# Expert tiles from the thirteenth on as float16 pairs, with the weights split on the chip

## The reference

```python
def attention(xn, Wq, Wk, Wv, Wb, Wg, Wo, norm_w):      # 4 heads, DK 128, DV 64
    q, k, v = xn @ Wq, xn @ Wk, xn @ Wv
    beta = sigmoid(xn @ Wb)
    k = k * rsqrt(sum(k * k) + 1e-12); q = q * SCALE
    # per token: pred = k_t S; S += k_t (beta_t (v_t - pred)); o_t = q_t S
    o = delta_rule(q, k, v, beta)
    o = o * rsqrt(mean(o * o) + 1e-5) * norm_w * silu(xn @ Wg)
    return o @ Wo

def ffn(xn, router_w, expert_fc, expert_proj):          # 8 experts, hidden 1024
    e = argmax(softmax(xn @ router_w.T))                # one expert for a token
    h = square(relu(xn @ expert_fc[e]))
    return h @ expert_proj[e].T

out = x + attention(xn) * silu(ffn(xn))
```

## Time and profile before

| | |
|---|---|
| median of 3 runs | 779.52 us (777.28 to 780.23) |
| profiled execution, its own time | 778.46 us |
| its span, first to last instruction | 776.7 us |
| TensorE busy | 729.9 us, 94% |
| VectorE busy | 537.6 us, 69% |
| GpSimd busy | 359.7 us, 46% |
| ScalarE busy | 356.5 us, 46% |

### The profile page before, as it was taken

How to read it: one execution, slowest core, us unless ns; L and a number is a source line. 1 busy time by engine, 2 the same in 40 slices (tenths; PEclk the granted TensorE clock), 3 DMA queues, 4 the chain that set the end, 5 groups by cost and what they waited for, 6 DMA issues and landing times.

```text
span 776.7 us, 22979 instructions
## 1 busy us (share of the span) xinstructions
PE 729.9 (94%) x9442; PEld 625.4 (81%) x9442; DVE 537.6 (69%) x1137; ACT 356.5 (46%) x768; POOL 359.7 (46%) x380
## 2 busy tenths in 40 slices
PE   5986999999999999999999999999999999999996
PEld 4764888878888788887978878888888888979873
DVE  6998156565665666646666586867777767777788
ACT  5922435444454444544445444444444353535532
POOL 5745126355353553535535272636354544426431
PEclk9988999999999999999999999999999999999999
DMA  8517853334433344333543333333333333323157
GB/s 295 182 55 271 301 191 150 149 130 151 190 132 135 131 176 173 142 118 130 193 154 144 116 138 110 130 117 124 124 124 123 123 124 123 118 110 118 36 179 263
DMA packets 37753, 116.33 MB, mean 150 GB/s; under 512 B 3664, under 2 KB 24400, under 8 KB 27664
## 3 DMA queue, kind: packets, MB, share of 16 engines
q1 hardware_dynamic: 33904, 104.62, 36.3%
q0 software_dynamic: 3744, 10.23, 4.2%
HBM read 101.33 MB, written 13.50 MB: 148 GB/s over the span
## 4 chain that ended last, share of the span: by engine, by line
PE 78%; DVE 11%; issue 4%; ACT 3%; DMA 2%; POOL 1%; DVEq 0%; SPq 0%; POOLq 0%
PE bank L521 18%; PE bank L510 16%; PE bank L556 5%; PE bank L590 5%; PE bank L484 4%; PE bank L486 4%; PE bank L485 4%; PE bank L731 3%; PE bank L540 3%; PE bank L638 3%; PE bank L647 3%; PE bank L629 3%; DVE Pm L1784 2%; PE bank L569 2%; DMA xs<-xn_d,from_row 1%
## 5 line engine op out<-in xcount | busy, mean ns | idle before, releaser
L521 PE MATMUL bank<-wts,hT 128*128 128x256 f32 x624 | 179.0, 397 | 0.0
L510 PE MATMUL bank<-xsT,wts 128*128 128x128 f32 x1248 | 173.7, 284 | 0.0
L510 PEld LDWEIGHTS bank<-xsT,wts 128*128 128x128 f32 x1248 | 154.3, 193 | 1.3
L2436 POOL TENSOR_TENSOR y_sb<-y_sb,y_sg 128x256 f32<-128x256 f32 x39 | 30.9, 801 | 181.3 <-ACT y_sg L1191 181.3
L1798 DVE TENSOR_TENSOR Pm<-bank,lvl_mask 128x256 f16<-128x256 f32 x180 | 68.0, 417 | 65.6 <-PE bank L629 65.6
L521 PEld LDWEIGHTS bank<-wts,hT 128*128 128x128 f32 x624 | 102.7, 191 | 5.6
L1227 ACT CAST Z<-bank 128x256 f16<-128x256 f32 x180 | 60.3, 376 | 96.4 <-PE bank L647 96.2
L1809 DVE TENSOR_TENSOR M<-bank,M 128x256 f16<-128x256 f32 x180 | 69.3, 419 | 44.4 <-PE bank L638 44.1
L1172 ACT ACTIVATE hT<-bank 128x512 f32<-128x512 f32 x78 | 47.0, 602 | 75.0 <-PE bank L510 74.2
L2469 POOL TENSOR_TENSOR PTl<-f_t,PTh 128x512 f16<-128x512 f32 x32 | 37.7, 1187 | 82.0 <-DVE PTh L1771 81.8
L2457 POOL TENSOR_TENSOR k16l<-f_t,k16h 128x512 f16<-128x512 f32 x32 | 38.5, 1205 | 41.6 <-DVE k16h L1721 41.6
(11 more groups left out here) (254 smaller groups left out, 1919.1 us busy)
## 6 DMA issues: line engine op xcount, KB each, us to landing
wts<-in_fc SPq DMA_DIRECT2D x39, 1024.0 KB, 5.0
wts<-in_pj SPq DMA_DIRECT2D x39, 1024.0 KB, 7.9
wts<-in_x SPq DMA_DIRECT2D x10, 512.0 KB, 7.9
wts<-y_d SPq DMA_DIRECT2D x4, 1024.0 KB, 9.4
out_x<-wts SPq DMA_DIRECT2D x16, 256.0 KB, 2.9
xn_d<-wts SPq DMA_DIRECT2D x3, 1024.0 KB, 4.4
x_first<-in_x SPq DMA_DIRECT2D x4, 512.0 KB, 11.7
wts<-in_x SPq DMA_DIRECT2D x4, 256.0 KB, 3.2
```

Of the source, the lines that this page charges most:

```text
L510: ins = pe.matmul(psum[bank[n]][:, (c % 4) * P:(c % 4 + 1) * P], fcw[r][:, k, c * P:(c + 1) * P], xsT[:, k, :], start=(k == 0), stop=(k == ...
L521: ins = pe.matmul(psum[bank[0]][:, 0:D], hT[:, c, :], pjw[r][:, c, :], start=(c == 0), stop=(c == HC - 1))
```

## The change

Tiles 0 to 11 stay float32. From tile 12 on, both products are made of float16 pairs, as in attention: 48 matmuls of 128x128 for the first and 24 of 128x256 for the second.

```diff
+T16 = 12
-        FIRST_TILES, STEPS = 3, [3] * 7 + [2] * 5
+        FIRST_TILES, FIRST_STEP, STEPS = 12, 4, [3] * 4 + [2] * 5
+        w16_d = scratch("w16_d", [E, P, 2, 2, KC * HD], F16)
...
                         for k in range(KC):
+                            if j < T16:
+                                ins = pe.matmul(o, fcw[r][:, k, c * P:(c + 1) * P], xsT[:, k, :],
+                                                start=(k == 0), stop=(k == KC - 1))
+                            else:
+                                ins = pairs(o, [fcw16[r][:, z, k, c * P:(c + 1) * P] for z in range(2)],
+                                            [xsT16[:, z, k, :] for z in range(2)], start=(k == 0), stop=(k == KC - 1))
...
+                    if j >= T16:
+                        n = 0
+                        for zh in range(2):
+                            for c in range(HC):
...
+                                for zw in range(2 - zh):
...
+                                    ins = pe.matmul(psum[bank[0]][:, 0:D], h16[:, zh, c, :], pjw16[r][:, zw, c, :],
+                                                    start=(n == 0), stop=(n == 3 * HC - 1))
```

```diff
+                def unit_load(u):
+                    if u < 2:
+                        act.wait_ge(wl_ok, W_ORDER[("wk", "wq")[u]])
+                    else:
+                        act.wait_ge(unit_lo, u - 1)
+                    act.dma_start(unit_in[u % 2], unit_of(u)[0]).then_inc(unit_read[u % 2], 16)
+
+                def unit_high(u):
+                    act.wait_ge(unit_read[u % 2], 16 * (u // 2 + 1))
...
+                        act.wait_ge(unit_kept[u % 2], 16 * (u // 2))
+                    act.activation(unit_out[u % 2][:, 0], unit_in[u % 2], ACT.Copy, scale=W_SCALE).then_inc(unit_hi, 1)
+
+                def unit_store(u):
+                    act.wait_ge(unit_lo, u + 1)
+                    act.dma_start(unit_of(u)[1], unit_out[u % 2]).then_inc(unit_kept[u % 2], 16)
...
+                def unit_low(u):
+                    dve.wait_ge(unit_hi, u + 1)
+                    dve.scalar_tensor_tensor(out=unit_out[u % 2][:, 1], in0=unit_in[u % 2], scalar=W_SCALE,
+                                             in1=unit_out[u % 2][:, 0], op0=ALU.mult, op1=ALU.subtract).then_inc(unit_lo, 1)
```

For a tile of the new kind ScalarE makes the square twice, as float16 (`h_high`) and as float32 (`sq`), GpSimd subtracts them (`h_low`), and VectorE makes the low half of the rows:

```diff
+                def h_high(j, n):
+                    At(act, j).on(relu_ok[n])
+                    act.activation(h16[:, 0, 4 * n:4 * n + 4, :].rearrange("p c n -> p (c n)"), half(n), ACT.Square,
+                                   scale=H_SCALE).then_inc(hh_ok[n], 1)
...
+                def h_low(j, n):
+                    At(pool, j).on(sq_ok[n])
+                    pool.wait_ge(hh_ok[n], HH_FROM[n] + j - T16 + 1)
+                    cs = slice(4 * n, 4 * n + 4)
+                    pool.tensor_tensor(h16[:, 1, cs, :], hT[:, cs, :], h16[:, 0, cs, :], ALU.subtract).then_inc(hl_ok[n], 1)
```

More of the change, by code:

```diff
@@ new lines, in ramp @@
+                    T(1, 3)
+                    KS(1)
+                    L(1, 4)
+                    G(2, 1)
+                    Dm(1, 4)
+                    experts(2)
+                    T(1, 4)
+                    experts(2)
+                    L(1, 5)
+                    K(3, 0)
+                    Q(3, 0)
+                    Dm(1, 5)
+                    experts(2)
+                    T(1, 5)
+                    F(1)
+                    PTm(2, 1)
+                    Zc(1)
+                    experts(6)
@@ new lines, in ramp @@
+                    U(1)
+                    experts(1)
+                    K(3, 1)
+                    experts(4)
+                    M0(2)
+                    O(1)
+                    experts(3)
+                    L(2, 0)
+                    experts(3)
+                    Dm(2, 0)
+                    experts(1)
+                    dS(1)
+                    T(2, 0)
+                    Q(3, 1)
+                    L(2, 1)
+                    experts(5)
+                    Dm(2, 1)
@@ new lines, in ramp @@
+                    T(2, 3)
+                    experts(3)
+                    L(2, 4)
+                    experts(2)
+                    Dm(2, 4)
+                    G(3, 0)
+                    PTm(3, 1)
+                    T(2, 4)
+                    Q(4, 0)
+                    L(2, 5)
+                    experts(2)
+                    wo(1)
+                    experts(2)
+                    Dm(2, 5)
+                    PTm(3, 0)
+                    KS(2)
+                    T(2, 5)
@@ new lines, in ramp @@
+                    experts(1)
+                    F(2)
+                    experts(2)
+                    Zc(2)
+                    K(4, 1)
+                    U(2)
+                    experts(2)
+                    K(4, 0)
+                    experts(3)
+                    O(2)
+                    experts(1)
+                    M0(3)
+                    experts(7)
+                    L(3, 0)
+                    Q(4, 1)
+                    Dm(3, 0)
+                    experts(2)
@@ new lines, in ramp @@
+                    L(3, 3)
+                    experts(3)
+                    Dm(3, 3)
+                    experts(2)
+                    kT(4, 0)
+                    T(3, 3)
+                    G(4, 1)
+                    ogT_(2)
+                    L(3, 4)
+                    VG(4, 1)
+                    Dm(3, 4)
+                    experts(2)
+                    G(4, 0)
+                    T(3, 4)
+                    experts(2)
+                    PTm(4, 1)
+                    L(3, 5)
```

2097 lines of the change are left out of this document (1398 added, 699 removed).

## The result

The changed kernel takes 766.05 us (median; 764.26 to 766.95) against 779.03 before: ratio 0.9834, 95% interval 0.9813 to 0.9854. It is faster by 1.7%. The forecast was 735, with 714 to 763 as its range, so the gain is 13 us where 44 were expected.

The account below looks back on a forecast made before the run. TensorE was taken as the bound in the steps and most of the ramp after 80 us. 778.46 - 62 + 7 + 4.8 + 2 + 2 + 2 = 734.3, plus 1.06 for the median: 735 us; forecast 726 to 745 (0.45), range 714 to 763.

Parts of the forecast that it names:

- The in-order coupling in the rest of the ramp: Ramp: in-order engines and 32 waits for units' landings add 2 us, bounds 0 and 30.
- The start, +7: Before the first gathered rows: 12.4 us extra on ScalarE makes logits about 7 us late, bounds 0 and 12.4.
- Work moved behind the rows' wait, +4.8: Ramp: TensorE work moved from its idle wait for gathered rows to behind the first tile's transposes adds 4.8 us.
- The tile's saving, 2.3 us: Expert tiles: float16 pairs save 2.35 us a tile, taken as 2.3; 27 tiles save 62 us.
- The weight load stays hidden: Experts' 128x128 float16 matmuls: weight loads don't set the pace, so they start 0.0555 us apart.
- rival C: Experts' float16 matmuls: weight loads set the pace at 99 ns, tiles save 7 us for 62; 790 us, chance 0.03.
- No engine becomes the bound in the steps, +2: Steps: added ScalarE, GpSimd and VectorE work hides under TensorE; 2 us over nine steps, bounds 0 to 12.
- Rival B: Steps or ramp: late pieces of in-order ScalarE stop TensorE, 0.75 us a unit; 759 us, chance 0.23 shared with another rival.
- The issues, 0.4 us each: ScalarE's queue: each unit DMA issue takes 0.4 us, upper end 0.87; twelve ahead of the logits make 4.8 us.
- The tail, +2: Tail: the last three chunks' chain may keep part of 11.5 us saved there; adds 2 us, bounds 0 and 6.
- Rival D: ScalarE: high halves wait for the store before last; slower than before from 1.4 us a unit, 799 at 2; chance 0.04.

Follow-up runs that it names:

- experiment 4: The change plus one wait: VectorE holds the tail's weighing from chunk 9 until GpSimd's last multiplication is done; 764.25 us.
- experiment 5: The change with the old order, casts on VectorE, up to the twelfth tile, no units, and stand-in weights; 721.22 us.
- the first experiment: The change without any splitting of weights into units (no load, cast, subtraction or store), stand-in weights, new order kept; 743.96 us.
- 2: The change with the units' high and low halves kept but their loads and stores left out, stand-in weights; 754.16 us.
- (6): Real weights on the old order up to the twelfth tile, 32 units 5.0 us apart, pairs from the thirteenth tile, tail's wait added; 757.02 us.
- The third experiment: The change with the six casts moved from ScalarE back to VectorE, each right behind what makes its input; 813.77 us.
- The twelfth kernel: The eighth kernel with the units' 64 loads and stores issued from SyncE's queue in place of ScalarE's; 742.16 us.
- seventh: Kernel (6) with float16 pairs only from the sixteenth tile and units 6.5 us apart; 750.78 us.
- eighth: The seventh kernel with a unit's halves side by side in the scratch, so stores write 4 KB rows for 2 KB; 749.67 us.
- tenth: The seventh kernel with low halves 1.2 us later on VectorE, and stores and next loads 1.2 us later on ScalarE; 750.62 us.

## Why the prediction was wrong

**The step that failed** is the term "The in-order coupling in the rest of the ramp, with 32 waits for landings: **+2**, bounds 0 and 30". In its place the units cost 22.1 us, 10.2 by their work and 11.9 by their transfers (the start's share is in it). The two other terms of the start and the ramp, +7 and +4.8, were too small as well: the new order alone, without any unit, costs 22.7. And the sum has no term for TensorE's clock, which fell from 0.94 to 0.81 in the start and from 0.99 to 0.95 in the ramp. Medians of the experiments split the time:

| | us |
|---|---|
| before, less 62 for 27 tiles | 717.0 |
| GpSimd's last product, stretched (4) | + 4.7 |
| the new order of start and ramp (5 to 1) | + 22.7 |
| the units' work (1 to 2) | + 10.2 |
| the units' transfers (2 to the change) | + 11.9 |
| sum | 766.5 |

against 766.05 measured. The first line is an estimate from the forecast's rate, the second from a profile, the others are differences of medians, which lead from the fifth kernel's 721.2 to 766.05 whatever they measure. So the sum tests only its first two lines, 721.7 for 721.2, and that this fits so well is partly luck: in the steps a tile saves 2.5 us for 2.3, and the five tiles of the tail save less. Nor are the parts fixed prices. In the order of before the same units cost 39 us (6) for 22 in the new order, so of a kernel with units the old order takes off some 5 us only: 757.0 against 766.05 less the 3 to 5 of the tail's wait.

- *The tile's saving, 2.3 us.* Right, a little low. (The prediction says that no float16 matmul of 256 columns is in the trace; there are two single ones, lines 451 and 463, which give no pace.) The chunk copy (line 1541 now) comes at 342.08 and 382.29, 40.2 us apart in steps of three tiles (forecast 41.2), and 35.2 in steps of two (35.7). A tile saves 2.5 to 2.6. In TensorE's timeline nine of the 256-column matmuls stand from 673.00 to 673.98, 0.109 each, and the 128x128 behind them start 56 ns apart:

```profile
673.00 1.15 PE L566 MATMUL bank<-wts,h 128*128 128x256 f16 x9
673.98 0.22 PE L517 MATMUL bank<-xsT,wts 128*128 128x128 f16 x1
674.03 0.22 PE L518 MATMUL bank<-xsT,wts 128*128 128x128 f16 x1
674.09 0.22 PE L519 MATMUL bank<-xsT,wts 128*128 128x128 f16 x1
```

- *The weight load stays hidden (against rival C).* Right. The Trainium skill, "TensorE: Matmul & The Clock Gate", section "Back-to-back issue gap", would have given 81 ns for each of these matmuls and kept the first product at 3.9 us; here 48 of them a tile, through the 22 tiles of the steps, start 56 apart.
- *No engine becomes the bound in the steps, +2.* Right: 1.6 us idle. ScalarE's busy time is 489 (forecast about 500). The third experiment shows how near it was in this order: with the casts on VectorE the cover is gone.
- *The start, +7.* Half of what came, and for a reason only partly mine. I put the 12.4 us of extra work on ScalarE ahead of the logits and took off its idle time. The logits came 15.3 us late; without any units they still are 9.6 late (54.35 for 44.79). There the last two low halves of x (VectorE) come from 49.95 on in place of 42.51. Between 15 and 54 us VectorE waits for high halves of x for 6.3 us in 4 places, and ScalarE for TensorE's transposes for 6.1 in 4. I read this as waits of the three engines for each other, which the new order made, and not as the sum of work on one; no run tests it. TensorE was busy for 18.9 of the 27 us from 15 to 42, in place of 24.2, and its clock was 0.78 (0.87 without units) in place of 1.00:

```profile
15.00:42.00 27.00, 18.91 (x167) 13.81 (x166) 22.25 (x62) 21.66 (x40) 18.60 (x26) 0.78 0.77 258
```

- *Work moved behind the rows' wait, +4.8.* Of about the right size for what it counted. TensorE is busy 9.4 us longer in the ramp of the first experiment than in the fifth's; the clock, 0.97 for 0.99, is some 3.6 of that (an estimate, 2% of 179 us). The 9 us of idle time had no term: in that ramp TensorE waits 3.9 us for VectorE's M, 3.3 for ScalarE's hT, 2.5 for R_l and 1.8 for GpSimd's k16l.
- *The coupling, +2.* Here both errors of method lie. I compared sums of busy time ("room") and the mean round of a buffer, 8 to 10.3 us for some 15 between a buffer's units. But a landing of median 4 to 6 us reached 11.6 and 13.1, in the weight loads' bursts. The trace of before had a warning that the prediction left out when it took 5.6 for a landing. Others of 0.5 MB in the same view as the earlier trace rows:

```profile
x_first<-in_wvg SPq DMA_DIRECT2D x1, 512.0 KB, 9.5
x_first<-in_x SPq DMA_DIRECT2D x4, 512.0 KB, 11.7
```

  And in an order a unit's delay isn't absorbed by room elsewhere: what stands behind it and is needed by TensorE now, as that Z, is late as well. The upper bound, 30, was near: 35.5 with the order's share. Rival B named this ("ScalarE, 76% asked for, is in order, and its late pieces stop TensorE; 32 units at 0.75 us"), at 759; measured were 22 us of 32 units, 0.69 each, in the change. Its price was right and its chance, 0.23, too small; what no rival had was the cost of the order alone, and the clock.
- *The issues, 0.4 us each.* The size is right (medians 0.36 and 0.40), the verdict not. From the Trainium skill, "DMA: Bandwidth & Descriptors", section "Issuing engines are not separate DMA queues", I had taken that only sequencer time is at stake and that it is usually small. The twelfth kernel moves the same 64 transfers to another engine's queue and gains 7.5 us. With a loaded, in-order engine the place of an issue matters; whether by its sequencer time, by its waits or by the landings is not shown.
- *The tail, +2.* It kept 11.5 - 5.6 = 5.9. 4.7 of that is GpSimd's stretched product (experiment 4). I had only looked at whether VectorE's work there would be the same, not at what it collides with when the chunk chain ends at another moment.

Rival D's mechanism (a high half stands until the store before last has landed) happened, on the chain itself, at half the price at which it would have decided.

## What to carry to other kernels

A task strewn into the orders of busy in-order engines should be priced by what stands behind each of its waits, and those waits by the longest landing in the trace and not by a short one; sums of busy time say only that it can fit. Idle time that it puts into TensorE can cost twice, once by itself and once through the clock. Try its DMAs in the queue of an engine that has little urgent behind them. When a change comes with a rewritten order, time the order without the task and the task in the old order: here each half cost over 20 us, together they hid nearly three quarters of a 62 us gain, and neither price held in the other's company.

## What the runs showed of the hardware

- GpSimd's multiplication of 128x512 with both inputs in SBUF took 1.04 us beside an idle VectorE and 6.04 beside an unbroken row of VectorE's instructions with two SBUF inputs; a wait in VectorE's order brought it back to 1.04. The Trainium skill, "SBUF — State Buffer", section "SBUF: two separate sides", has the two engines lock a shared pair of ports for a whole instruction, and "the other fully blocks". The trace agrees, and adds that the lock did not pass over between VectorE's instructions: GpSimd waited through all that were left, some eight. In the kernel before it was GpSimd that came first: its product took 1.13, and three of VectorE's multiplications behind it 2.73 in place of 1.88. The units' low halves, with two inputs in SBUF too, took 1.22 us (median) in the change and up to 3.02 beside GpSimd's work.
- Between 80 and 280 us, while SyncE's queue loaded 2 MB of weights a tile, a 0.5 MB store issued by ScalarE landed after 7.8 and 7.4 us (median) in the seventh and eighth kernels, but after 5.7 in the tenth and 4.3 in the change; in SyncE's own queue, in the twelfth, after 4.9. So the moment of issue moved it as much as the queue may have; no run separates the two.
- 128x128 float16 matmuls with a weight load each started 56 ns apart, 128x256 109, through the 22 tiles of the steps, where TensorE was idle for 1.6 of 334.6 us.
- With the same matmuls, TensorE was busy for 169.9 us at a granted clock of 0.99 and 4.1 us of idle time (experiment 5), and for 190.2 at 0.91 and 25.9 us of idle time (6).
